# Two-layer network on one core: keys and queries turned by products with a rounded identity, and the bias row of the summary scores as one product

## What is computed

```python
def reference(x, ...):
    xn = _layernorm(x)
    x = x + _L0_attn_ref(xn, ...) + _L0_ffn_ref(xn, ...)
    xn = _layernorm(x)
    return x + _L1_attn_ref(xn, ...) + _L1_ffn_ref(xn, ...)

def _L0_attn_ref(x, Wq, bq, Wk, bk, Wv, bv, Wo, bo):     # 16 heads of 64, a summary each 64 rows
    summary = ...                                         # 32 means of 64 rows
    q = (x @ Wq + bq)...; k = (summary @ Wk + bk)...; v = (summary @ Wv + bv)...
    scores = jnp.einsum('bhtd,bhcd->bhtc', q, k) * scale
    scores = jnp.where(allowed[None, None], scores, -jnp.inf)
    out = jnp.einsum('bhtc,bhcd->bhtd', softmax(scores), v)
    return out... @ Wo + bo

def _L0_ffn_ref(x, ...):                                  # 16 query heads, 4 key groups, head size 8
    h = rmsnorm(x, ln1_w)
    q, k, v = h @ Wq + bq, h @ Wk + bk, h @ Wv + bv
    q, k = rmsnorm(apply_rope(q), qn_w), rmsnorm(apply_rope(k), kn_w)
    scores = jnp.einsum('bthd,bshd->bhts', q, k) / np.sqrt(HD)      # causal, 2048 x 2048
    out = jnp.einsum('bhts,bshd->bthd', softmax(scores), v)
    gate = sigmoid(out @ Wg + bg)
    x = x + (out * gate) @ Wo + bo
    ...                                                   # top-1 of 8 experts, added to x
```

## Time and profile before

| | |
|---|---|
| median of three runs | 604.74 us (603.96 to 604.87) |
| profiled execution | 600.14 us, span 598.2 us |
| PE busy | 560.7 us, 94% of the span |
| ACT busy | 468.7 us, 78% |
| DVE busy | 400.2 us, 67% |
| POOL busy | 123.8 us, 21% |
| granted clock of PE | 1.00 on average over the span |

### The profile page before, as it was taken

How to read it: one execution, slowest core, us unless ns; L and a number is a source line. 1 busy time by engine, 2 the same in 40 slices (tenths; PEclk the granted TensorE clock), 3 DMA queues, 4 the chain that set the end, 5 groups by cost and what they waited for, 6 DMA issues and landing times.

```text
span 598.2 us, 11222 instructions
## 1 busy us (share of the span) xinstructions
PE 560.7 (94%) x3939; PEld 330.1 (55%) x3939; DVE 400.2 (67%) x1059; ACT 468.7 (78%) x664; POOL 123.8 (21%) x161
## 2 busy tenths in 40 slices
PE   6799999999999999999988799797799999999998
PEld 3343333443443434333435487385578887887887
DVE  6784887666273454586527555887888798698773
ACT  5599999999999999999967265479597686785673
POOL 2063321020020021003701655112012010020010
DMA  7112001035222220300325220200000000000000
GB/s 227 41 29 67 2 24 49 1 94 160 94 108 90 97 82 2 112 32 12 114 83 183 76 72 37 83 2 0 1 1 2 1 18 1 2 18 1 2 19 18
DMA packets 30982, 30.72 MB, mean 51 GB/s; under 512 B 6848, under 2 KB 20960, under 8 KB 30928
## 3 DMA queue, kind: packets, MB, share of 16 engines
q1 hardware_dynamic: 29680, 27.45, 14.6%
q0 software_dynamic: 1248, 2.57, 1.2%
HBM read 13.44 MB, written 12.89 MB: 44 GB/s over the span
## 4 chain that ended last, share of the span: by engine, by line
PE 69%; DVE 15%; ACT 6%; issue 6%; DMA 3%; POOL 1%; SPq 0%; DVEq 0%; ACTq 0%; POOLq 0%
PE ps L1402 18%; PE ps L1381 9%; PE ps L92 6%; PE ps L94 6%; PE ps L93 6%; PE ps L1705 2%; ACT r L997 2%; PE ps L1482 2%; PE ps L1580 1%; PE ps L1295 1%; PE ps L1743 1%; PE ps L1746 1%; PE ps L1255 1%; PE ps L1474 1%; PE ps L1710 1%
## 5 line engine op out<-in xcount | busy, mean ns | idle before, releaser
L997 ACT ACTIVATE r<-ps 128x1024 f32<-128x1024 f32 x272 | 257.3, 1040 | 16.4 <-PE ps L1381 14.2
L1402 PE MATMUL ps<-r 128*32 128x512 f32 (+3 forms) x1280 | 144.8, 539 | 1.0 <-DVE r L2139 0.6
L853 POOL TENSOR_SCALAR_AFFINE_SELECT r<-r 128x512 f32<-128x512 f32 (+1 forms) x80 | 47.0, 589 | 206.3 <-ACT r L997 206.0
L1381 PE MATMUL ps<-r2r 32*128 32x512 f32 (+3 forms) x640 | 79.2, 445 | 2.1 <-ACT r L997 1.3
L1381 PEld LDWEIGHTS ps<-r2r 32*128 32x128 f32 x640 | 35.5, 182 | 43.8 <-issue 19.0
L896 POOL TENSOR_TENSOR r<-r 128x512 f32<-128x512 f32 x16 | 22.7, 1416 | 151.0 <-ACT r L1198 130.1
L1402 PEld LDWEIGHTS ps<-r 128*32 128x32 f32 x1280 | 27.8, 108 | 40.4 <-issue 26.9
L94 PE MATMUL ps<-r2r 128*128 128x512 f32 (+1 forms) x104 | 39.1, 376 | 0.0
L1267 PE MATMUL ps<-consts 128*128 128x512 bf16 x99 | 25.6, 398 | 8.2 <-DMA consts<-in_consts 4.2
L93 PE MATMUL ps<-r2r 128*128 128x512 f32 (+1 forms) x88 | 32.8, 372 | 0.0
L831 POOL DMA_INDIRECT rows_by_expert<-r x16 | 17.8, 1115 | 54.9 <-DVE r L2062 51.1
(11 more groups left out here) (419 smaller groups left out, 1194.6 us busy)
## 6 DMA issues: line engine op xcount, KB each, us to landing
rows_by_expert<-r SPq DMA_DIRECT2D x34, 258.0 KB, 2.5
r2r<-r2r SPq DMA_DIRECT2D x56, 64.0 KB, 2.0
r<-in_f_W SPq DMA_DIRECT2D x1, 2048.0 KB, 9.2
r<-rows_by_expert SPq DMA_DIRECT2D x23, 64.5 KB, 1.9
res<-in_x SPq DMA_DIRECT2D x4, 256.0 KB, 3.8
r<-in_g_h1T SPq DMA_DIRECT2D x1, 1024.0 KB, 6.5
r<-in_g_h2T SPq DMA_DIRECT2D x1, 1024.0 KB, 8.2
r<-rows_by_token SPq DMA_DIRECT2D x4, 256.0 KB, 4.0
```

Source lines behind the costliest of these rows:

```text
L853: pool.affine_select(blk, blk, pattern, ALU.is_ge, nothing, base=0, channel_multiplier=-1).then_inc(s_msk, 1)
L997: act.activation(probs[:, n % PBUFS, :, :], ps[:, b:b + 2, :], ACT.Exp).then_inc(s_exp, 1)
L1381: m = pe.matmul(ps[:, 2 * (n % SBUFS) + h, at:at + TB - query], kst[32 * j:32 * j + 32, group, P * kt:P * kt + P], qst[32 * j:32 * j + 32, ...
L1402: m = pe.matmul(ps[32 * j:32 * j + 32, 6, query:TB], vp[:, kt, group, :], probs[:, (2 * v + j // 2) % PBUFS, j % 2, at:at + TB - query], s ...
```

## The change

It has three parts. (A) The turning of keys and queries is no longer a transpose but a product with `identr`, the identity rounded to the format fp32r; the tiles, which hold parts already in that format, are read as fp32r. POOL makes the copy once at the start, and PE's wait for POOL's first preparations (`s_pad` at 2) moves up in front of the first turning of keys. (B) The bias row G0 is one float32 product of 128 x 512: ones times `kbd`, which DVE has multiplied in place by bq0 after its copy of GMAT. The release of the shared bank after GMAT now comes after that multiplication. (C) The table asks for G0 one step after GMAT's end with a gap (2 steps), for one step in place of four, and for VW from step 42, after G0.

```diff
+        identr = r3r[:, 9728:9856]
...
-            + [... (26, 4, "GMAT", 0, ("KV", 0), 2), (31, 4, "G0", 0, ("KV", 0), 2),
-               (36, 2, "VW", 0, ("KV", 0), 1)]
+            + [... (26, 4, "GMAT", 0, ("KV", 0), 2), (31, 1, "G0", 0, ("GMAT", 0), 2),
+               (42, 2, "VW", 0, ("G0", 0), 1)]
...
+            step.alone(pool.tensor_copy(identr, ident))
             pool.sem_inc(s_pad, 1)
...
-                    m = pe.transpose(ps[:, bank, P * i:P * i + P], khl_f[:, i].rearrange("p g s r d -> p (g s r d)"),
-                                     ident)
+                    m = pe.matmul(ps[:, bank, P * i:P * i + P], khl[:, i].rearrange("p g s r d -> p (g s r d)"),
+                                  identr, start=True, stop=True)
...
-                    src = qhl_f[:, i, REP * g:REP * g + REP].rearrange("p j r s d -> p (j r s d)")
-                    m = pe.transpose(ps[:, bank, P * i:P * i + P], src, ident)
+                    src = qhl[:, i, REP * g:REP * g + REP].rearrange("p j r s d -> p (j r s d)")
+                    m = pe.matmul(ps[:, bank, P * i:P * i + P], src, identr, start=True, stop=True)
...
+            pe.wait_ge(s_pad, 2)
             keys_transposed(4).then_inc(s_kt, 1)
...
             pe.wait_ge(s_kc, 1)
-            pe.wait_ge(s_pad, 2)
...
-                    elif what in ("GMAT", "G0"):
+                    elif what == "GMAT":
                         pe.wait_ge(s_kbd, 1)
                         for j in share(HC):
-                            w = wqT[:, j, :] if what == "GMAT" else bq0[:, j:j + 1].broadcast_to([P, P])
-                            a = pe.matmul(ps[:, SHARED, 64 * j:64 * j + 64], w,
+                            a = pe.matmul(ps[:, SHARED, 64 * j:64 * j + 64], wqT[:, j, :],
                                           kbd[:, j].rearrange("p a c -> p (a c)"), start=True, stop=True)
+                    elif what == "G0":
+                        a = pe.matmul(ps[:, SHARED, :], ones, kbd.rearrange("p j a c -> p (j a c)"), start=True, stop=True)
...
-                    dve.tensor_copy(dst.rearrange("p a b -> p (a b)"), bank).then_inc(s_mr, 1)
+                    if what == "GMAT":
+                        kbd_j = kbd.rearrange("p j a c -> p j (a c)")
+                        step.mark(dve.tensor_copy(dst.rearrange("p a b -> p (a b)"), bank))
+                        step.mark(dve.tensor_tensor(kbd_j, kbd_j, over(bq0, 64), ALU.mult))
+                        step.settle()
+                        dve.sem_inc(s_mr, 1)
+                    else:
+                        dve.tensor_copy(dst.rearrange("p a b -> p (a b)"), bank).then_inc(s_mr, 1)
```

More of the change, by code:

```diff
@@ L546, in build @@
                ((1, (8, 12, 15.5, 19)), (2, (25.6, 33, 45, 52)), (3, (65, 74, 89, 102))) for g, at in enumerate(steps)]
-            + [(27, 1, "KVROWS", 0, ("KEYS", 2), 0), (27, 1, "KV", 0, ("KVROWS", 0), 2), (26, 4, "GMAT", 0, ("KV", 0), 2), (31, 4, "G0", 0, ("KV", 0), 2),
-               (36, 2, "VW", 0, ("KV", 0), 1)]
+            + [(27, 1, "KVROWS", 0, ("KEYS", 2), 0), (27, 1, "KV", 0, ("KVROWS", 0), 2), (26, 4, "GMAT", 0, ("KV", 0), 2), (31, 1, "G0", 0, ("GMAT", 0), 2),
+               (42, 2, "VW", 0, ("G0", 0), 1)]
             + [(LAST[r] + LAG + 1, 2 if r[1] else 1, "ATT", r, None, 0) for r in PAIRED]
```

## The result

| | before | after |
|---|---|---|
| median of four executions each | 604.48 us (603.96 to 604.87) | 610.3 us (609.81 to 611.73) |
| ratio, 95% interval | | 1.0102 (1.0077 to 1.0128) |
| profiled execution, span | 598.2 us | 607.9 us |
| mean granted clock of PE in the profiled execution | 1.00 | 0.98 |
| idle time of ACT before its exponentials | 16.4 us | 25.2 us |

The kernel is slower by 5.8 us (a fourth execution of before, 604.21 us, has joined the three shown ahead); 606.0 was forecast, 603.3 to 607.2 as the range. The page of the profile after gives the slices of the clock (PEclk, tenths of full speed), and the groups of the value products and of the exponentials (columns: busy us, mean ns, idle before and what ended most of it).

The account below looks back on a forecast made before the run. The attention stage was taken as bound by ACT's exponentials, and by PE where late with scores. Terms 0 − 0.5 − 0.6 + 0.1 + 2.3 = +1.3 us on 604.7 gave 606.0 us, range 603.3 to 607.2.

Parts of the forecast that it names:

- Bound: Attention stage: bound by ACT's exponentials, and by PE where it is late with scores; 14.2 of 16.4 us idle.
- Part A at 0: Turning of keys and queries: four fp32r products take 0.58 us like four transposes, so twenty groups change nothing.
- Rival 2: Turning products cost the float32 price, 0.51 us more per group; the sum above 611 us; chance 0.04.
- Part B at −0.5: G0 as one product of 1.05 us in place of four parts totalling 2.36: −0.5 us, between −0.1 and −1.3.
- the working's own bound of −0.15: G0: PE's overrun of ACT's step time falls from 0.8 to 0.65 us, which alone gives −0.15.
- Three freed steps let later pieces move up: Steps no longer holding parts of G0 were to advance later pieces, a gain counted within −0.5 us.
- Part C at −0.6: Table from SCORE 0 on: pieces get other neighbours and two waits of PE for DVE go, −0.6 us.
- Both waits of PE: PE's waits for DVE ahead of TRANSPOSE 0 (0.37 us) and TRANSPOSE 7 (0.20 us), claimed to go.
- The multiplication at +0.1: DVE's multiplication, 0.68 us, delays the shared bank's release after GMAT: +0.1 us, from 0 to 0.7.
- Rival 3: SCORE 0 also waits, since DVE's work behind G0 barely fits: PE waits about 1 us more, 607.0 us; chance 0.10.
- The new wait at +2.3: Copy of bank 6 falls behind SCORE 7's train and best_expert: PE stalls 3.3 us, ACT dry 2.1 to 2.7; +2.3.
- −1.3 − 0.6 + 0.1: Not-slower rival, chance 0.24: pieces save all PE saved; with the stall gone altogether, given as −1.9 us, 602.8.

Follow-up runs that it names:

- the changed kernel's second profile: The changed kernel run again, its plan's lag written as 1 + 1, no other edit: 604.46 us against 600.55 for the kernel before, ratio 1.0070.
- the two kernels with another wait: Changed kernel with best_expert's five DVE instructions behind the copy of bank 6: 1.0058; kernel before with that copy done five times: 1.0063, repeated 1.0074.
- the fillers: Thirteen idle products put into PE's waits between 11 and 29 us, on the kernel before: 600.18 us, ratio 0.9998.

## Why the prediction was wrong

**Bound.** Right: ACT's idle time grew by 8.8 us (25.2 less 16.4) where the profiled span grew by 9.7, and where PE stood, ACT ran dry.

**Part A at 0.** Right for the engine: +0.1 us by steps for all twenty groups. The weight loads of the products take longer than the transposes' (median 189 ns and 140 ns), which the pitch, the time from one product's start to the next one's, hides. As a term of the time it was wrong: the kernels with products in the first five groups stand at 1.0022 to 1.0027, some 1.5 us, and one set of four at 1.0054. This goes with half clock, which the rows of one execution at full clock can't show. Rival 2, the float32 price, did not occur: a group takes 0.59 us (126.23 to 126.82 in the changed kernel's second profile) against 0.58. The Trainium skill ("TensorE: Matmul & The Clock Gate", Terms) gives the transpose mode as four times faster for FP32; against an fp32r product these rows show no such difference.

**Part B at −0.5.** Too large. The product took what GATE's row said (in the changed kernel's second profile):

```profile
111.00 1.12 PE L1460 MATMUL ps<-r,consts 128*128 128x512 f32 x2
112.06 0.50 PE L1383 MATMUL ps<-r2r 32*128 32x512 f32 x4
```

that is 1.06 us. By steps (in the kernel without part A), the first two steps without a part of G0 gain 0.13 and 0.20 us, and the one with the whole product is 0.45 longer than one that had a part, so 0.65 over ACT's pace of 1.82: that is the working's own bound of −0.15. "Three freed steps let later pieces move up" won nothing, and by step 107 the 0.15 is gone as well.

**Part C at −0.6.** This step failed. Both waits of PE went (TRANSPOSE 0 starts at 128.26 without idle time), but the time up to step 107 is the same within 0.02 us. The first wait did cost ACT something, and a new wait of PE took its place. ACT before, behind TRANSPOSE 0; then, in the changed kernel's second profile, PE at OT 0 and ACT behind it:

```profile
132.89 1.94 ACT L997 ACTIVATE r<-ps 128x1024 f32<-128x1024 f32 x2 [0.30 <-PE ps L1381]
...
135.78 0.66 PE L1494 MATMUL ps<-consts,r 128*128 128x128 f32 x4 [0.54 <-DVE res L2245]
...
136.91 5.61 ACT L999 ACTIVATE r<-ps 128x1024 f32<-128x1024 f32 x6 [0.16 <-PE ps L1383]
```

Where 0.30 us of ACT's idle time stood behind TRANSPOSE 0, there is 0.05 in the plan after, and the step is 0.26 us shorter (2.29 and 2.03). Three steps on, ahead of OT 0, PE now waits 0.54 us until DVE has read OUTPUT 0, and that step is 0.28 us longer (2.34 and 2.62). ACT's losses at SCORE 1 and OUTPUT 0, 0.41 and 0.59 us before and 0.42 and 0.60 after, stand wherever these pieces stand. The working counted the waits that go and not those that come. TRANSPOSE 7 lies behind step 109, where its 0.20 can't be told from the rest.

**The multiplication at +0.1.** Right: 0.07 us is missing from the first freed step's gain (0.13 against 0.20). Rival 3 did not come.

**The new wait at +2.3.** The mechanism, place and order were right. The wait is 2.46 us in place of 3.3: 0.44 of the difference is the cast in SCORE 7's train (0.21 us and not the 0.65 of that one execution), 0.17 the product in front of it (0.70 and not 0.87). But all of it is paid, since PE has no lead there: ACT is short of scores by 0.23 and 0.36 us in the two steps ahead of it. By the two kernels with another wait (1.06 us with 0.98, 2.87 with 2.81) it is an estimated 2.5 us, near the term. What is missing in the forecast is the **half clock behind it**, a term that it put at nothing without a word: what is left of the loss is 3.47 − 2.5 = 1.0 us with the short stretch and 4.79 − 2.5 = 2.3 with the long one.

**The sum.** Forecast −0.5 − 0.6 + 0.1 + 2.3 = +1.3. In its place stand 0.0 up to step 107, +2.5 for the wait, +1.0 to +2.3 for the clock behind it, +0.1 for part A, which is 3.6 to 4.9; with some 1.5 for the clock at the start, 5.1 to 6.4 at most. Measured were +5.8 beside the first runs of before and +3.9 in the second comparison (604.46 against 600.55). The two terms of −1.1 (B and C), of which nothing was left, took the forecast to the edge of no change; without them it would have been 607.1, just inside its range. The clock, which had no term, put the result outside. That the first comparison came to 5.8 and not 3.9 is open, as said above. Two small slips of the prediction change nothing: −1.3 − 0.6 + 0.1 is −1.8 (602.9), and its terms give 605.0 to 606.8 as the forecast's own range.

## What to carry to other kernels

Where a plan is moved, look for the one copy that gates the next round and for what is bound to other events and now falls in front of it: here a train of six instructions moved in front of it and a chore of five kept its old place, together they made the loss, and four numbers of a table took it away. Count as a gain only what the engine that bounds the stage was idle for, and look through the new order for waits that come as well as for those that go. And price a stop of PE with what its clock may do behind it.

## What the runs showed of the hardware

- With a stop of 2.46 us the granted clock fell to 1.2 GHz for 3.4 to 6.8 us in three profiles of the changed plan, from 0.4 us before PE went on to 1.5 us after it; with one of 2.80 or 2.81 us in the other plan it stayed at 2.4 GHz twice. PE had run without idle time for over 2 us ahead of each stop.
- One program can have its clock at 2.4 GHz throughout or at 1.2 GHz for some 10 us early in the span (before: none in one profile, 3.4 us at 18.4 and 6.8 at 32.1 in the next). With the stretch at 32 us 2.6 us were lost up to step 6, with one of 13.7 us in another kernel 3.5; the fillers in PE's waits did not change before's median.
- With products in place of transposes in the first five turnings 24 of 28 executions had a mean clock of 0.991 or lower, with transposes there 4 of 24.
- A product of 128 columns in fp32r by an identity and a float32 transpose of the same tile have the same pitch (0.11 us, and 0.58 to 0.59 for a group of four), though the weights take 189 and 140 ns to load.
